# Two PSUM banks in place of three for projections, v and routing, and a third bank for the transposed scores

## The reference

```python
xn = (x - mu) * rsqrt(var + 1e-5) * gamma + beta          # of layernorm(x)
q, k = xn @ Wq + bq, xn @ Wk + bk                         # 8 heads, dk = 16
v = (xn @ Wv + bv).reshape(B, S, H, D)
p = softmax(einsum('bhsd,bhtd->bhst', q, k) / sqrt(dk))
att = einsum('bhst,bhtd->bhsd', p, v)
x = x + att.reshape(S, B, D, H).sum(-1).reshape(B, S, D)  # groups of 8 columns summed
u = layernorm(x)                                          # 8192 tokens
gates = sigmoid(u @ centroids.T); keep the top 2, divide by their sum
h = gelu(einsum('nd,edf->enf', u, W1) + b1)               # d_ff = 512
x = x + einsum('ne,end->nd', gates, einsum('enf,efd->end', h, W2) + b2)
```

## Time and profile before

| | |
|---|---|
| median of 3 runs | 947.78 us (940.97 to 954.12) |
| span of the profiled execution | 938.7 us; the page gives no other time of it |
| TensorE matmul busy | 663.7 us, 71% |
| VectorE busy | 618.0 us, 66% |
| GpSimd busy | 586.2 us, 62% |
| ScalarE busy | 490.2 us, 52% |
| mean granted TensorE clock | 0.844 |

### The profile page before, as it was taken

The page is one execution under the profiler, slowest core; times in us unless marked ns, Lnnn a source line. Parts: engine busy times, 40 slices in busy tenths (PEclk is TensorE's granted clock), DMA queues, the critical chain, the costliest instruction groups (busy, mean ns, idle before and its releaser), DMA issues. The chain is left out here.

```text
span 938.7 us, 15215 instructions
## 1 busy us (share of the span) xinstructions
PE 663.7 (71%) x3889; PEld 493.0 (53%) x3889; DVE 618.0 (66%) x1662; ACT 490.2 (52%) x901; POOL 586.2 (62%) x602
## 2 busy tenths in 40 slices
PE   3799877878878788885108767767677776677750
PEld 1467655656656556653106555555565655565540
DVE  5578877667667775664407886787576776867640
ACT  4278765666666666454106555455454554545520
POOL 4433565565466555546722778786777777767885
PEclk9899997897798888779558899887887988978885
DMA  4998766665576657511173454545455445545320
GB/s 88 120 105 117 113 102 99 99 114 88 87 113 91 95 90 103 90 43 49 49 167 111 90 124 87 90 97 99 85 101 90 84 90 93 114 86 99 65 25 0
DMA packets 129830, 85.67 MB, mean 91 GB/s; under 512 B 20088, under 2 KB 122496, under 8 KB 129792
## 3 DMA queue, kind: packets, MB, share of 16 engines
q1 hardware_dynamic: 100608, 66.95, 39.6%
q0 software_dynamic: 26560, 16.96, 13.6%
q10 hardware_dynamic: 2624, 1.33, 0.7%
HBM read 36.23 MB, written 25.33 MB: 66 GB/s over the span
## 5 line engine op out<-in xcount | busy, mean ns | idle before, releaser
L573 POOL DMA_INDIRECT out_dram<-probs,gate_row x156 | 256.1, 1642 | 52.4 <-issue 49.3
L928 DVE TENSOR_REDUCE row_max<-ps_max 128x2 f32<-128x512 f32 x256 | 174.5, 687 | 122.2 <-PE ps_max L734 60.1
L600 ACT ACTIVATE probs<-ps_st 128x512 f32<-128x512 f32 x256 | 147.4, 595 | 137.1 <-PE ps_st L746 95.7
L734 PE MATMUL ps_max<-k_stack,q_stack 96*128 96x256 f32 x512 | 144.0, 369 | 64.0 <-DVE row_max L928 57.7
L1119 DVE TENSOR_TENSOR k_stack<-probs,k_stack 128x512 fp32r<-128x512 f32 x156 | 136.4, 874 | 69.9 <-ACT k_stack L704 68.1
L734 PEld LDWEIGHTS ps_max<-k_stack,q_stack 96*128 96x128 f32 x512 | 90.2, 217 | 121.2 <-DVE row_max L928 84.9
L856 PE MATMUL ps_max<-k_stack,q_stack 128*128 128x512 f32 x156 | 72.3, 464 | 107.8 <-issue 76.6
L530 POOL DMA_INDIRECT slots<-y_row,slot_idx x128 | 125.7, 982 | 36.0 <-issue 34.8
L746 PE MATMUL ps_st<-q_stack,k_stack 128*128 128x256 f32 x512 | 115.1, 311 | 5.7 <-ACT probs L600 5.2
L701 ACT ACTIVATE probs<-ps_st,b_cur 128x512 f32<-128x512 f32 x78 | 53.9, 691 | 95.2 <-POOL b_cur L553 66.3
L856 PEld LDWEIGHTS ps_max<-k_stack,q_stack 128*128 128x128 f32 x156 | 33.3, 213 | 128.1 <-issue 122.0
(11 more groups left out here) (154 smaller groups left out, 1399.7 us busy)
## 6 DMA issues: line engine op xcount, KB each, us to landing
probs<-in_L_ffn_W_dram SPq DMA_DIRECT2D x78, 256.0 KB
probs<-slots SPq DMA_DIRECT2D x39, 260.0 KB, 3.0
q_stack<-q_hi SPq DMA_DIRECT2D x64, 128.0 KB
k_stack<-k_hi SPq DMA_DIRECT2D x64, 128.0 KB
X<-in_L_attn_x_dram SPq DMA_DIRECT2D x16, 256.0 KB, 5.0
q_stack<-q_lo SPq DMA_DIRECT2D x32, 128.0 KB
k_stack<-k_lo SPq DMA_DIRECT2D x32, 128.0 KB
out_dram<-X SPq DMA_DIRECT2D x32, 128.0 KB
```

The costliest lines, as they stand in the source:

```text
L573: pool.indirect_dma_start(out_rows, bass.IndirectOffsetOnAxis(gate_row[r][:, c, 1:2].bitcast(I32), 0), res[par][:, c * P:(c + 1) * P], Non ...
L600: act.activation(probs[slot % 2][:, h, :, :], ps_st[h % 2][:], ACT.Exp, scale=DK ** -0.5).then_inc(exp_done, 1)
L734: last = pe.matmul(ps_max[k % 2][:, hh, :], q_stack[slot][0:M_ROW, h, sc * P:(sc + 1) * P], k_stack[slot][0:M_ROW, h, :], start=True, stop ...
L928: dve.tensor_reduce(row_max[slot % 2][:, sc, 2 * hp:2 * hp + 2], ps_max[k % 2][:], AX.X, ALU.max).then_inc(smax_reduced, 1)
```

## The change

The bank `ps_mv` is gone. `ps_route` becomes `ps_small`, in which the transposed row maxima, the logits and the rank counts have columns of their own; the v products and the transposed y go to `ps_proj`. The eighth bank becomes a third `ps_st`. The steps are put in another order, since products that share a bank must wait for each other's readers:

- The transposed scores take bank (8 slot + k) mod 3, and wait for the exp three units back (two back for the first two units of slot 0, where the ring of 32 units closes).
- v products: from even k = 4 to odd k = 0 of the next period, behind the logits; the addition on VectorE from even k = 6 to odd k = 1.
- Rank: from even k = 2 to k = 3; its reading from k = 3 to k = 4.
- Transposed row maxima: in odd periods from k = 1 to k = 2, and ScalarE's copy and DMA with them (h = 1 and 2 become h = 2 and 3). In even periods the copy and the DMA come ahead of the y and k steps of their unit.
- The exp of the logits on ScalarE comes at h = 0, before the z activations, in place of h = 1.
- New waits on TensorE guard the shared banks.

```diff
-        ps_st = [ctx.enter_context(nc.psum_tensor(f"ps_st{n}", [P, 2, S], F32)) for n in range(2)]
+        ps_st = [ctx.enter_context(nc.psum_tensor(f"ps_st{n}", [P, 2, S], F32)) for n in range(3)]
...
-        ps_mv = ctx.enter_context(nc.psum_tensor("ps_mv", [P, 512], F32))
-        ps_route = ctx.enter_context(nc.psum_tensor("ps_route", [P, 512], F32))
+        ps_small = ctx.enter_context(nc.psum_tensor("ps_small", [P, 512], F32))
+        ps_maxT = ps_small[0:H, 0:S]
+        ps_logits = ps_small[:, S:S + 4 * E]
+        ps_rank = ps_small[:, S + 4 * E:S + 9 * E]
...
+        def bank(slot, k):
+            return (8 * slot + k) % 3, 2 if slot == 0 and k < 2 else 3
...
-        ps_h = [ps_st[n][:].rearrange("p a s -> p (a s)") for n in range(2)] + [ps_proj[:], ps_mv[:]]
+        ps_h = [ps_st[n][:].rearrange("p a s -> p (a s)") for n in range(2)] + [ps_proj[:], ps_st[2][:].rearrange("p a s -> p (a s)")]
...
-                    act.activation(probs[slot % 2][:, h, :, :], ps_st[h % 2][:], ACT.Exp,
+                    act.activation(probs[slot % 2][:, h, :, :], ps_st[bank(slot, h)[0]][:], ACT.Exp,
...
+                    if h == 0 and rl:
+                        wait(act, logits_ready, rl[0] + 1)
+                        wait(act, gating, GATING * rl[0])
+                        act.activation(expn[:], ps_logits.rearrange("p (c e) -> p c e", e=E), ACT.Exp,
+                                       scale=-1.0).then_inc(expn_ready, 1)
+                    if h == (2 if t.odd else 1) and t.batch(1):
+                        b, bi, slot = t.batch(1)
+                        wait(act, maxT_ready, b + 1)
+                        if not (t.fixed and b < 2):
+                            o = slot - 2
+                            act.wait_ge(m_placed[o % 4], 16 * (bi + o // 4 + 1))
+                        act.activation(neg_maxT[slot % 2][:], ps_maxT, ACT.Copy, scale=-1.0).then_inc(neg_maxT_ready, 1)
+                    if h == (3 if t.odd else 2) and t.batch(1):
+                        b, bi, slot = t.batch(1)
+                        wait(act, neg_maxT_ready, b + 1)
+                        act.wait_ge(stack_placed[slot], 96 * (bi + 1))
+                        act.dma_start(q_stack[slot][M_ROW:M_ROW + 1, :, :].rearrange("p h s -> p (h s)").bitcast(F32),
+                                      neg_maxT[slot % 2][:].bitcast(F32)).then_inc(m_placed[slot], 16)
...
-                    if h == 1 and rl:
...
-                    if h == 1 and t.batch(1):
...
-                    if h == 2 and t.batch(1):
...
-                        act.activation(yT[:], ps_route[:], ACT.Copy).then_inc(yT_ready, 1)
+                        act.activation(yT[:], ps_proj[:], ACT.Copy).then_inc(yT_ready, 1)
...
-                    wait(pe, exp_done, 8 * b + h - 1)
+                    place, depth = bank(slot, h)
+                    wait(pe, exp_done, 8 * b + h + 1 - depth)
...
-                        last = pe.matmul(ps_st[h % 2][:, tc, :], k_stack[slot][:, h, tc * P:(tc + 1) * P],
+                        last = pe.matmul(ps_st[place][:, tc, :], k_stack[slot][:, h, tc * P:(tc + 1) * P],
...
-                prep_v = None if t.odd else t.pair(0)
+                prep_v = t.pair(-1) if t.odd else None
...
-                    if k == 1 and t.batch(1):
+                    if k == (2 if t.odd else 1) and t.batch(1):
...
+                        if t.fixed and b == 0:
+                            pe.wait_ge(centT_ready, 1)
+                        if t.odd and t.pair(-9):
+                            wait(pe, filled, t.pair(-9)[0] + 1)
+                        if logits_n:
+                            wait(pe, expn_ready, logits_n[0] + 1)
...
-                        if t.odd and t.pair(-1):
-                            wait(pe, v_ready, t.pair(-1)[0] + 1)
...
-                            last = pe.transpose(ps_mv[0:H, sc * P:(sc + 1) * P], row_max[slot % 2][:, sc, :], ident[:])
+                            last = pe.transpose(ps_maxT[:, sc * P:(sc + 1) * P], row_max[slot % 2][:, sc, :], ident[:])
...
-                    if k == 2 and rank_n:
+                    if k == 3 and rank_n:
...
-                        rank = ps_route[:, 0:5 * E]
+                        wait(pe, filled, rank_n[0])
+                        if t.batch(1):
+                            wait(pe, neg_maxT_ready, t.batch(1)[0] + 1)
+                        rank = ps_rank
...
+                        if prep_v:
+                            wait(pe, v_ready, prep_v[0] + 1)
...
-                        if rank_n:
-                            wait(pe, filled, rank_n[0] + 1)
-                        elif ny > 0:
-                            wait(pe, expn_ready, ny)
+                        if prep_k:
+                            wait(pe, k_hi_ready, prep_k[0] + 1)
+                        elif t.pair(0):
+                            wait(pe, v_ready, t.pair(0)[0])
...
-                            last = pe.transpose(ps_route[:, c * P:(c + 1) * P], y_row[py][0][:, c, 0:D], ident[:])
+                            last = pe.transpose(ps_proj[:, c * P:(c + 1) * P], y_row[py][0][:, c, 0:D], ident[:])
...
+                        wait(pe, expn_ready, logits_n[0])
+                        if t.pair(-9):
+                            wait(pe, filled, t.pair(-9)[0] + 1)
+                        if t.batch(2):
+                            wait(pe, neg_maxT_ready, t.batch(2)[0] + 1)
...
-                            last = pe.matmul(ps_route[:, c * E:(c + 1) * E], yT[:, c * P:(c + 1) * P], centT[:],
+                            last = pe.matmul(ps_logits[:, c * E:(c + 1) * E], yT[:, c * P:(c + 1) * P], centT[:],
...
-                    if k == 4 and prep_v:
+                    if k == 0 and prep_v:
...
-                        if t.batch(1):
-                            wait(pe, neg_maxT_ready, t.batch(1)[0] + 1)
+                        if logits_n:
+                            wait(pe, yT_ready, logits_n[0] + 1)
+                        elif t.pair(1):
+                            wait(pe, k_hi_ready, t.pair(1)[0] + 1)
...
-                            last = pe.matmul(ps_mv[:, c * P:(c + 1) * P], xnT[par][:, c * P:(c + 1) * P], Wv_s[:],
+                            last = pe.matmul(ps_proj[:, c * P:(c + 1) * P], xnT[par][:, c * P:(c + 1) * P], Wv_s[:],
...
-                if k == 3:
+                if k == 4:
...
-                prep_v = None if t.odd else t.pair(0)
+                prep_v = t.pair(-1) if t.odd else None
...
-                    if k == 6 and prep_v:
+                    if k == 1 and prep_v:
...
-                                          ps_mv[:].rearrange("p (c h d) -> p c h d", c=4, h=H),
+                                          ps_proj[:].rearrange("p (c h d) -> p c h d", c=4, h=H),
...
```

More of the change, by code:

```diff
@@ L294, in build @@
         h_lo = [[cols(k_stack[2 + n], f, 1) for f in range(FC)] for n in range(2)]
-        ps_h = [ps_st[n][:].rearrange("p a s -> p (a s)") for n in range(2)] + [ps_proj[:], ps_mv[:]]
+        ps_h = [ps_st[n][:].rearrange("p a s -> p (a s)") for n in range(2)] + [ps_proj[:], ps_st[2][:].rearrange("p a s -> p (a s)")]
         ps_o = [ps_max[n][:].rearrange("p a s -> p (a s)") for n in range(2)]
         ps_y = ps_av[:].rearrange("p a s -> p (a s)")
-        ps_t = ps_route[:]
+        ps_t = ps_small[:]
         class Step:
@@ L584, in _ @@
             act.wait_ge(centT_psum, 1)
-            act.activation(centT[:], ps_route[:, 0:E], ACT.Copy).then_inc(centT_ready, 1)
+            act.activation(centT[:], ps_small[:, 0:E], ACT.Copy).then_inc(centT_ready, 1)
             act.wait_ge(qk_loaded, 4 * 16)
@@ L632, in body @@
                             last.then_inc(y_ready, 1)
-                    if h == 1 and rl:
-                        wait(act, logits_ready, rl[0] + 1)
-                        wait(act, gating, GATING * rl[0])
-                        act.activation(expn[:], ps_route[:, 0:4 * E].rearrange("p (c e) -> p c e", e=E), ACT.Exp,
-                                       scale=-1.0).then_inc(expn_ready, 1)
-                    if h == 1 and t.batch(1):
-                        b, bi, slot = t.batch(1)
-                        wait(act, maxT_ready, b + 1)
-                        if not (t.fixed and b < 2):
-                            o = slot - 2
-                            act.wait_ge(m_placed[o % 4], 16 * (bi + o // 4 + 1))
-                        act.activation(neg_maxT[slot % 2][:], ps_mv[0:H, 0:S], ACT.Copy, scale=-1.0).then_inc(neg_maxT_ready, 1)
-                    if h == 2 and t.batch(1):
-                        b, bi, slot = t.batch(1)
-                        wait(act, neg_maxT_ready, b + 1)
-                        act.wait_ge(stack_placed[slot], 96 * (bi + 1))
-                        act.dma_start(q_stack[slot][M_ROW:M_ROW + 1, :, :].rearrange("p h s -> p (h s)").bitcast(F32),
-                                      neg_maxT[slot % 2][:].bitcast(F32)).then_inc(m_placed[slot], 16)
                     if h == 2 and prep_k:
```

(4 more changed lines are left out.)

## The result

The changed kernel takes 953.99 us (median of 20 runs, 949.72 to 962.79), the kernel before 945.33 us beside it (20 runs, 940.53 to 954.12): a ratio of 1.010, 95% interval 1.0078 to 1.0122. The time forecast was 955.3. The profiled execution spans 952.3 us against 938.7, 13.6 more, where the medians differ by 8.7: the twenty runs of the changed kernel are 1.6 to 2.0 us longer than their spans, so the profiled execution of the kernel before took about 940.4 us, some 5 less than the median of its kernel, and that of the changed kernel, 953.97, stands at its median.

A forecast was written before the change was run, and what follows sets the result against it. TensorE's results were held until row scatters end, once in nearly every period, then a reduction chain follows. -1 + 6.0 + 2.5 + 0 + 0 = +7.5 us; 938.7 + 7.5 + 9.1 = 955.3, range 932 to 972.

The forecast's parts named there:

- Part 1: Third transposed-score bank: removes only TensorE's waits for ScalarE's exp; -1 us, bounds 0 and -7.6.
- Part 4: VectorE: v's addition moves to odd unit 1, two rank reads to unit 4; covered, 0, bound -8.3 us.
- Part 3: Clock: TensorE's longer pause before even unit 5 makes two to three more even periods slow; +2.5 us, bounds 0 and +6.
- Part 5: Small moves of rank, row-max transposes, their copy and DMA, logit exp and new waits: hidden, 0, bounds -2 and +2 us.
- Part 2: v products into odd unit 0: nothing saved in even periods, six low-clock odd ones pay 1.0 us each; +6.0, bounds 0 and +18.8.
- the 9.1 us: Gap between the profiled span, 938.7 us, and the median of the runs, 947.78, added to the forecast as time around the span.
- rival 1: Clearly slower: v paid in full in every odd period, 18.8 us, plus 5 for the clock: 970.6 us; chance 0.22.
- the move is neutral: Early periods, TensorE nearly full: moving v takes 1.06 us from the even period and adds it to the odd one.
- Rival 2: Faster: VectorE's relief reaches the scatters (-8.3), third bank takes all its waits (-7.6), clock held (-6): 926 us; chance 0.20.
- Rival 3: Nothing moves: the release sets both kinds of period and all else fits under it; 945 to 950 us; chance 0.18.
- the release depends on TensorE's order: Sign of being wrong: VectorE's remote waits shrink or shift, and then all sums are off; no size given.
- a wait of the z transposes for v's addition: Sign of being wrong: the addition should be over 1 to 2 us before the z transposes' turn.

The follow-up runs named there:

- ring2: The changed kernel with the third transposed-score bank left unused, its ring two deep as before: 951.47 us, 1.0092 of the kernel before.
- max3: The changed kernel with the third bank given to the row-max scores and the transposed scores two deep again: 936.75 us.
- v_even: The changed kernel with a two-deep transposed-score ring and the v products back in even unit 4, in the bank this leaves idle: 940.87 us.
- max3_v_even: The kernel before, its order kept on TensorE and VectorE, with three row-max banks, v on the projection bank and one shared small bank: 863.92 us, 0.9905 of before.
- before_again: The kernel before, unchanged, run again as the scale for the level 870: 869.67 us.
- after_again: The changed kernel, unchanged, run again as the scale for the level 870: 892.3 us, 1.0262 of the kernel before.

## Why the prediction was right, and where it was not

The size was right (955.3 against 953.99) and the sign too; Part 1 held, and Part 4 for the even period. The rest of the agreement is luck in good part. Part 3 was too high and Part 5 too low, and they nearly cancelled. Part 2 came to its sum on a condition that did not hold. And the start was off: the 9.1 us kept "as what lies around the span" are 1.6 to 2.0 in the runs of the changed kernel, the rest being that the profiled execution was a short one; the median of three runs, 947.78, lay 2.5 above that of twenty, 945.33, while the change cost 8.7 us and not 7.5.

**Part 1, the third bank, -1: right.** The waits for the exp vanished and ring2 lies within its interval of the change. The argument, that the other ring holds TensorE, is what max3 shows. What the Trainium skill says of a repeated gap stands in its page Perfetto Trace Analysis under Optimization Strategy.

**Part 2, v: the sum was near (+6.0 forecast; +6.8 by eleven odd periods of 0.62; 4.2 by the 0.39 of ring2, which has the same order), its condition wrong.** "Saves nothing in the even period" held (13.81 to 13.86). But the step said "at full clock 0, at the low clock 1.0 us". Full-clock odd periods take 13.06 to 13.70 us where the one of before took 12.20, and odd ones below 0.8 take 13.4 to 15.8 where before had 12.9 to 13.9: both kinds pay. The odd period of the earlier trace rows, taken as one at full clock, has a mean of 0.87 in the earlier trace rows; the one at 1.00 is the 12.20 above. Nor was the price that of the logit records, 1.71 us: in odd unit 0 the v products take 1.14 us at the full clock and, in four of the eleven periods, 2.05 at the low one. The failed assumption is that the hold-up stays at its place and swallows what is put ahead of it. It moved to an earlier unit. Where there are no hold-ups (the level 870) an odd period grows by 1.18 us, v's full length of 1.14; at the level 943 it grows by 0.62, less than half of the mean length there (1.47). So rival 1 (v paid in every odd period) named the mechanism better than the forecast did; what it had too high is that each pays in full.

**Part 3, the clock, +2.5: did not happen.** TensorE's pause grew by 0.44 us in the mean and not by the 1.06 forecast, and the mean clock is 0.86 in both kernels in periods 8 to 30. Even periods gained 0.05 us, 0.6 over twelve. The Trainium skill (TensorE: Matmul & The Clock Gate, Why this matters for your kernels) ties idle gaps to half clock. The low stretches follow the pauses here as well, but a longer pause brought no more of them, and v_even, with shorter pauses (mean 1.46 us) and the lowest clock, is faster.

**Part 4, VectorE, 0: right for the even period.** Its length did not change at either level. For the odd one "covered" holds only with idle time on VectorE: at 229.37 the addition stands directly ahead of the next reduction, and the z transposes waited 0.2 us for it.

**Part 5, the small moves, 0: wrong.** The step said that the row of maxima "is needed only at the next period's unit 0, over 4 us later". That holds in the steady stretch, not in the early one. The row-max DMA of period 1 in the timeline of the kernel before:

```profile
40.37 1.26 ACTq L651 DMA_DIRECT2D q_stack<-neg_maxT  x1
```

The same DMA after the change:

```profile
41.89 1.25 ACTq L634 DMA_DIRECT2D q_stack<-neg_maxT  x1
```

And, among the waits of the changed kernel from 37 to 70 us:

```profile
PE ps_st L753 <- DMA q_stack<-neg_maxT: 2.3, 1, 2.3
```

The transposes stand behind v and one unit later, so the DMA starts 1.5 us later among SyncE's placements, and TensorE waits 2.3 us for it before the product at 49.1 us, falls to a lower clock, and period 2 takes 10.80 us instead of 8.60. Its row in the kernel before, with the columns of the earlier trace rows:

```profile
46.20:54.80 8.60, 7.92 (x61) 5.79 (x61) 7.52 (x20) 5.99 (x11) 3.71 (x4) 1.00 0.77 74
```

And of after:

```profile
46.30:57.10 10.80, 8.39 (x52) 6.33 (x52) 7.17 (x19) 5.95 (x12) 3.75 (x4) 0.84 0.61 59
```

That is 2.2 of the 3.8 us lost by period 8. The prediction's claim for these periods, "the move is neutral", failed with it. The cause is not settled: v_even and max3_v_even start this DMA at 40.20 and 40.27 us, earlier than before, and their TensorE waits 1.9 and 1.8 us for it all the same; with three quarters of v out, the two orders reach period 8 at 102.3 and 102.6. The late issue is at most one way to that wait. The trace adds that the DMA's last packet ends at 47.05 us in the changed kernel and at 46.42 in v_even, 2.1 and 2.6 us before TensorE goes on, against 44.83 in the kernel before. What delays the packets and the release was not tried.

So -1 + 6.0 + 2.5 + 0 + 0 = +7.5 became, in the span, about 0 + 6.8 + 0.6 + 0 + 3.8, and 2.4 in unchanged code. In the medians the difference is 8.7 us; which of these terms is smaller there, one trace of each kernel can't tell, but the loss before period 8 is there in the other pairs too (5.5 us for before_again and after_again, 5.7 without scatters).

**Rivals.** Rival 2 (faster) fell: even periods did not shorten, the clock did not rise, and the exp waits came off without gain. Rival 3 (nothing moves) is half true of even periods. The doubt kept in reserve, "the release depends on TensorE's order", should have carried more weight: the remote waits kept their sum but moved within the odd period, just what that sentence calls wrong. The other sign of being wrong, a wait of the z transposes for v's addition, showed once, with 0.2 us.

## What to carry to other kernels

Before giving a bank to a ring, read which ring's semaphore the busiest engine waits for: at the level 943 the same bank was worth nothing on the exp ring and 1.5% on the row-max ring. A product is priced by the period it moves into: look for the slack of that period at the moved unit and ask whether the stall that should hide it stays in its place when the order changes. Where the work is an alternation of a full and a slack period, a move from the slack to the full one costs its whole length, and the first iterations of a pipeline, in which DMAs are densest, need their own line in the sum.

## What the runs showed of the hardware

- The same kernel takes 943 us in one group of runs and 870 in two others, and the change costs 1.0% at the one level and 2.6% at the other. One group of either level bears the chip number 12, so the chip alone is not shown to decide. At the level 943 the reductions wait 53.7 us, in 17 waits of up to 4.4, for a remote release; at 870 there is none from 100 to 350 us, and the clock is 0.99 there against 0.85 to 0.86.
- In a hold-up TensorE's finished work reaches the other engines one by one: in the odd period above the reduction of unit 1 starts at 228.76, ScalarE's exp at 230.18 and the reduction of unit 2 at 230.24, after idle times of 3.68, 3.54 and 0.19 us, though their products had all started by 226.7. In that one the release came 0.65 us after the last scatter's issue, in the even one 2.02, so the 2.1 to 2.25 us of the prediction are no constant.
- A lower mean clock (v_even, 0.82) went with a shorter time than a higher one (ring2, 0.90): TensorE is busy 255.0 of the 296 us from 104 to 400 in v_even and 235.8 in ring2. Where TensorE waits in any case, a cold TensorE fills its waits.
